# Banded attention: where the softmax's exponential, negation and sum are done, head by head on ScalarE

## What is computed

```python
idx = jnp.arange(T)[:, None] - deltas[None, :]
valid = idx >= 0
k_mod = k[:, :, idxc] * (1.0 + scale_embed)
scores = jnp.einsum('bhtd,bhtjd->bhtj', q, k_mod) * scale + pos_bias.T[None, :, None, :]
scores = jnp.where(valid[None, None], scores, jnp.finfo(scores.dtype).min)
attn = jax.nn.softmax(scores, axis=-1)          # over the 42 offsets, for each of 16 heads
out = jnp.einsum('bhtj,bhtjd->bhtd', attn, v_g) * if_gain[None, :, None, None]
return out.transpose(0, 2, 1, 3).reshape(B, T, C) @ w_out
```

## Time and profile before

| what | us |
|---|---|
| median of three runs | 3405.57 (3402.1 to 3410.08) |
| the profiled execution's own time | 3413.12 |
| its span | 3411.2 |
| steps of chunk 0 | 21.4 to 70.4 |
| steps of chunk 1, with the tail of chunk 0 | 70.4 to 142.9 |
| steps of chunk 2, with the tail of chunk 1 | 142.9 to 215.1 |
| steps of chunk 3, with the tail of chunk 2 | 215.1 to 284.3 |
| tail of chunk 3 alone | 284.3 to about 330 |

### The profile page before, as it was taken

How to read it: one execution, slowest core, us unless ns; L and a number is a source line. 1 busy time by engine, 2 the same in 40 slices (tenths; PEclk the granted TensorE clock), 3 DMA queues, 4 the chain that set the end, 5 groups by cost and what they waited for, 6 DMA issues and landing times. The chain is left out here.

```text
span 3411.2 us, 72275 instructions
## 1 busy us (share of the span) xinstructions
PE 3068.7 (90%) x29076; PEld 2124.1 (62%) x29076; DVE 1814.2 (53%) x4513; ACT 1181.2 (35%) x2319; POOL 995.6 (29%) x822
## 2 busy tenths in 40 slices
PE   8997999999988888889678999699997999889989
PEld 3434555555667865658345555489997886666656
DVE  7897544453334655433776666543333763455543
ACT  1223333332233431313326665222222652244433
POOL 1001443343102111426248878321111211104001
PEclk9998999999998999989889999799998999999989
DMA  4223000000222022527211110378886200121100
GB/s 156 65 75 100 10 9 18 9 9 0 54 58 26 7 52 74 150 79 255 70 33 31 32 31 19 110 292 329 328 328 230 77 2 13 37 73 51 49 14 19
DMA packets 174741, 287.70 MB, mean 84 GB/s; under 512 B 79393, under 2 KB 145025, under 8 KB 165102
## 3 DMA queue, kind: packets, MB, share of 16 engines
q1 hardware_dynamic: 166958, 263.07, 24.0%
q0 software_dynamic: 7488, 20.46, 1.8%
HBM read 245.07 MB, written 28.48 MB: 80 GB/s over the span
## 5 line engine op out<-in xcount | busy, mean ns | idle before, releaser
L2852 PE MATMUL ps<-L_ffn_xsT,arena 128*128 128x128 f32 x2584 | 304.0, 276 | 0.7 <-DVE L_ffn_xsT L2651 0.6
L2852 PEld LDWEIGHTS ps<-L_ffn_xsT,arena 128*128 128x128 f32 x2584 | 296.3, 193 | 3.6 <-DVE L_ffn_xsT L2651 3.5
L842 POOL TENSOR_TENSOR L_xattn_rn<-L_xattn_ss,mhalf 125x16 f32<-125x16 f32 (+1 forms) x64 | 185.8, 2903 | 257.3 <-DVE L_xattn_ss L905 257.3
L3534 POOL TENSOR_TENSOR L_xattn_pT<-L_xattn_pT,L_xattn_keep 125x678 int32<-125x678 int32 x128 | 190.4, 1509 | 62.6 <-ACT L_xattn_pT L3789 62.6
L162 POOL TENSOR_TENSOR rstd<-nsc,mhalf 112x4 f32<-112x4 f32 (+2 forms) x26 | 40.2, 1545 | 556.0 <-DVE nsc L155 555.0
L2750 ACT ACTIVATE L_ffn_silu<-ps,arena 128x128 f32<-128x128 f32 x280 | 102.9, 368 | 269.2 <-PE ps L2852 254.0
L2660 DVE SCALAR_TENSOR_TENSOR L_ffn_hT<-ps,arena,L_ffn_silu 128x128 f32<-128x128 f32 x280 | 98.0, 350 | 155.3 <-ACT L_ffn_silu L2750 155.1
L2529 POOL DMA_INDIRECT L_ffn_rows_out<-L_ffn_ys,L_ffn_dest x78 | 79.6, 1021 | 319.8 <-DVE L_ffn_ys L2669 304.1
L1019 PE MATMUL ps<-arena,L_xattn_cT 128*125 128x512 f32 x384 | 166.1, 592 | 0.0
L723 PE MATMUL ps<-L_attn_prod,arena 128*32 128x448 f32 (+28 forms) x672 | 153.5, 492 | 11.5 <-DVE L_attn_prod L523 10.9
L2865 PE MATMUL ps<-arena,L_ffn_hT 128*128 128x256 f32 x646 | 153.0, 381 | 5.5 <-ACT L_ffn_ys L2759 5.4
(11 more groups left out here) (616 smaller groups left out, 6753.2 us busy)
## 6 DMA issues: line engine op xcount, KB each, us to landing
arena<-in_L_ffn_up SPq DMA_DIRECT2D x35, 2056.0 KB, 8.1
arena<-in_L_ffn_down SPq DMA_DIRECT2D x35, 1152.0 KB, 8.6
L_xattn_ctxT<-in_ctxT SPq DMA_DIRECT2D x48, 375.0 KB, 3.7
arena<-in_L_ffn_up SPq DMA_DIRECT2D x43, 384.0 KB, 4.5
L_attn_a<-L_attn_skew SPq DMA_DIRECT2D x16, 784.0 KB, 5.2
L_xattn_ctx<-in_ctx SPq DMA_DIRECT2D x30, 375.0 KB
arena<-L_xattn_kp SPq DMA_DIRECT2D x64, 93.8 KB, 3.3
L_xattn_mask<-in_mask SPq DMA_DIRECT2D x32, 164.1 KB, 8.4
```

The costliest lines, as they stand in the source:

```text
L842: nc.gpsimd.tensor_tensor(rn[0:r, i], ss[0:r, i], core.mhalf[0:r, 0:H], ALU.pow).then_inc(po_r.step("root", i), 1)
L2852: ins = nc.tensor.matmul(ps[:, 2 + b % 4, half * TS:(half + 1) * TS], self.up(i % WU, k, half * HM + m), xsT[:, i % 2, k], start=(k == 0), ...
L3534: nc.gpsimd.tensor_tensor(p, p, keep[:, n % 2].unsqueeze(1).to_broadcast([SP_, 2, ST * TP]), ALU.mult).then_inc(po_e.step("kept", half), 1)
```

## The change

In the tails of chunks 0, 1 and 2 the subtraction over 672 elements is replaced by a negation of the 16 maxima. ACT takes the exponential as 16 instructions, one for each head, of 42 elements that lie 16 apart, with the negated maximum as bias and the sum accumulated into `den`. VectorE's sum is left out there. Before its first exponential of a chunk but the first, ACT waits for the reciprocal of the chunk before. `DIVIDE`, `TURN`, `ATTEND`, `SCALED`, `PROJECT` and `UPDATE` go four steps later, `MAX`, `SUB` and `EXP` stay. The last chunk's tail and its tables stay as they are.

```diff
-        ve_n = [Progress(core, f"vector_norm{u}", ("den", 1), ("rden", 1), ("wide", 1)) for u in range(U)]
+        ve_n = [Progress(core, f"vector_norm{u}", ("rden", 1), ("wide", 1)) for u in range(U)]
+        ve_f = [core.semaphore(f"vector_den{u}") for u in range(U)]
...
-            DIVIDE = {17 + 12 * u: u for u in range(U)}
-            TURN = {25 + 12 * (n // 4) + 2 * (n % 4): n for n in range(4 * U)}
-            ATTEND, SCALED, PROJECT = ({n + 12 * u: u for u in range(U)} for n in (33, 41, 42))
-            UPDATE = {min(50 + 12 * u, NI - 1): u for u in range(U)}
+            DIVIDE = {21 + 12 * u: u for u in range(U)}
+            TURN = {29 + 12 * (n // 4) + 2 * (n % 4): n for n in range(4 * U)}
+            ATTEND, SCALED, PROJECT = ({n + 12 * u: u for u in range(U)} for n in (37, 45, 46))
+            UPDATE = {min(54 + 12 * u, NI - 1): u for u in range(U)}
...
-                        dve.wait_ge(ve_n[u].sem, ve_n[u].at(c - 2, "den"))
+                        dve.wait_ge(ac_e.sem, ac_e.at(c - 2, "exp", u))
...
             def below(c, u):
                 dve.wait_ge(ve_m[u].sem, ve_m[u].at(c, "max"))
+                if c < NCH - 1:
+                    nc.vector.tensor_scalar(mx[:, u, :], mx[:, u, :], -1.0, None, ALU.mult).then_inc(ve_m[u].step("sub"), 1)
+                    return
...
                 dve.wait_ge(ac_e.sem, ac_e.at(c, "exp", u))
-                nc.vector.tensor_reduce(den[:, u, :], by_head(e[c % 2][:, u]), AX.X, ALU.add).then_inc(ve.step("den"), 1)
-                dve.wait_ge(ve.sem, ve.at(c, "den"))
+                if c < NCH - 1:
+                    core.stand(dve)
+                else:
+                    nc.vector.tensor_reduce(den[:, u, :], by_head(e[c % 2][:, u]), AX.X, ALU.add).then_inc(ve_f[u], 1)
+                    dve.wait_ge(ve_f[u], 1)
...
             def exponential(c, u):
                 act.wait_ge(ve_m[u].sem, ve_m[u].at(c, "sub"))
+                if c < NCH - 1:
+                    if c:
+                        act.wait_ge(ve_n[u].sem, ve_n[u].at(c - 1, "rden"))
+                    for h in range(H):
+                        row = by_head(e[c % 2][:, u])[:, h, :]
+                        ins = nc.scalar.activation(row, row, ACT.Exp, bias=mx[:, u, h:h + 1], accum_out=den[:, u, h:h + 1])
+                    ins.then_inc(ac_e.step("exp", u), 1)
+                    return
```

## The result

| | before | after |
|---|---|---|
| median of 5 runs, us | 3410.08 (3402.1 to 3415.9) | 3431.97 (3422.99 to 3437.66) |
| the profiled execution's own time, us | 3413.12 | 3422.99 |
| steps of chunk 1, us | 72.5 | 80.2 |
| steps of chunk 2, us | 72.2 | 81.2 |
| steps of chunk 3, us | 69.1 | 73.2 |

The ratio is 1.0061, with a 95% interval of 1.0045 to 1.0077: slower, by 21.9 us between the medians. The stage alone is 20.9 us longer (346.8 - 325.9). The two profiled executions differ by 9.9 us only, because stages that the change does not touch were some 11 us shorter in the profiled one of after; so from here on chunks and the end of the stage are compared, and ratios of medians where there are several runs.

The account below looks back on a forecast made before the run. PE and DVE were taken as nearly full, with faster DVE worth at most some 8.6 us each in chunks 1 and 2. Chunks sum 6.0 + 5.0 - 0.7 = 10.3 us more, 3416 forecast; range 3398 to 3429.

Parts of the forecast that it names:

- Price of a head: ACT, one activation of 42 spread elements plus accumulator read: 0.37 us (0.33 to 0.42); sixteen take 5.9 us.
- Step 1: Chunk 1: turned-input copies end at 88.6 behind the first exponential, so PE's q starts at 88.7 instead of 84.29.
- Step 2: Chunk 1: second exponential ends at 104.9, weight copies queue behind it, PE's third turn at 105.3 instead of 97.20.
- Step 3: Chunk 1, third turn to that of sequence 2: 22.1 us instead of 23.5; 1.4 of DVE's 5 us reach PE.
- Step 4: Chunk 1, sequence 2's third turn to next chunk's first product: 21.5 us instead of 22.2; chunk ends 6.0 later.
- Chunk 2: Same as chunk 1, but PE no longer lags into it, about 1 us back: 5.0 us later.
- Chunk 3: First exponential 10 us in, transfers 7.9, first turn some 24 in; 0.4 later on DVE, 1.1 less PE lag: -0.7.
- 1.1 less lag of PE: End of chunk 3: PE lags 1.1 us less, credited against 0.4 us later on DVE.
- Faster: DVE sets the pace: Exponentials hide and PE's waits on DVE in its own rows go: -10 us, 3395; chance 18%.
- Even: A head costs 0.33 us and the chain overstates adding waits: +2.6 or less, about 3408; chance 25%.
- Much slower: A head costs 0.42 us or more, accumulator reads not overlapping: +20, 3425, or beyond; chance 12%.
- signs: Activations about 0.28 us with reads between, q waiting on ACT, DVE waiting at `DIVIDE`, chunks 78, 77, about 70 us.

Follow-up runs that it names:

- version with right filling: Kernel after plus small constant products filling PE's stands: 16 before q, 8 before the third turn, in chunk 3 10 before the first turn; 1.0043, stage end 340.9.
- second profile of after: The kernel after run once more, unchanged, to see how far its stage repeats; ratio 1.0075, chunks of 80.3, 81.6 and 73.8, stage end 347.8.

## Why the prediction was wrong in size and right in direction

It said 10.3 us more, 3416; it came to 21.9 more, 3431.97, outside the range (3398 to 3429). Of the 16 us between these times 4.5 are before's own median, 3410.08 over five runs where the prediction had 3405.57 over three; with that median 21.9 more would have been 3427.5. The size is off all the same, 21.9 for 10.3. The stage gives 20.9.

What failed: the prediction let PE stand in front of q and of the turns and put the clock behind it at nothing, which was some 6 us; it took two credits, 1.0 for chunk 2 and 1.1 at the end, that did not come; and it had the first turn of chunk 3 too early. The cause of the slowdown, that ACT's exponentials stand in front of q and the weight copies, was right. By the steps of the text:

- **Price of a head**, 0.37 (0.33 to 0.42): 0.35, sixteen 5.6 where 5.9 stood. Right.
- **Step 1**, q at 88.7: 88.34, right in time. Missed: the clock. q took 3.19 us instead of 1.77, since PE had stood 3.95 us. The prediction wrote that PE stands and put no price on what follows.
- **Step 2**, third turn at 105.3: 106.08. In the version with right filling it came at 104.58, so the clock was 1.5 of it, and without the clock the step would have been 0.7 early (two exponentials at 5.6).
- **Step 3**, 22.1 us to the third turn of sequence 2: 22.3 (128.41). Of DVE's relief only a little reaches PE, as said. That the sum is so near is partly luck. From the end of the third exponential to the start of the fourth it took 6.8 us (115.17 to 122.00) where 5.9 stood, and the terms written there, 0.85, 0.58, 0.75, 1.04 and 1.8, make 5.0 only; shorter exponentials and a sooner last turn made up for it.
- **Step 4**, 21.5 us to the end, 2.5 of them waits of DVE: 22.2, with 0.78 + 0.62 + 1.94 = 3.3 of waits (22.8 in the version with right filling). Chunk 1 is 7.7 longer, not 6.0.
- **Chunk 2**, "PE no longer lags into it: about 1 us back": did not happen. The first exponential starts 11.0 us after the chunk's first product before and after, and the filled version's chunk 2 is 6.0 longer than before's, the sum without the credit. With the clock, lower for 6.8 + 3.4 us here, that makes 9.0 instead of 5.0.
- **Chunk 3**, +0.4 on DVE: +4.1. Wrong was the time of the first turn: "some 24 us in", measured 25.8. The first exponential starts 11.0 us in, before (226.03 - 215.06) and after, where the prediction read 10. And the transfers took longer: 9.2 us from the exponential's end to the first turn (257.62 - 248.39), where 7.9 stood. The score copy behind the first exponential, missed too, is not what held this turn: PE stood again, for the read back. ACT's timeline of the kernel before, the first exponential of chunk 3:

```profile
226.03 0.77 ACT L598 ACTIVATE arena<-arena 112x672 f32<-112x672 f32 x1
```

  SP's timeline of the kernel after and of before shows where the 1.3 went:

```profile
248.56 0.30 SPq L394 DMA_DIRECT2D L_attn_skew<-arena  x1
248.92 0.42 SPq L395 DMA_DIRECT2D L_attn_skew<-arena  x1
252.64 0.30 SPq L401 DMA_DIRECT2D L_attn_a<-L_attn_skew  x1
```

```profile
227.22 0.42 SPq L394 DMA_DIRECT2D L_attn_skew<-arena  x1
229.66 0.30 SPq L400 DMA_DIRECT2D L_attn_a<-L_attn_skew  x1
```

  The read back follows the second write to the skewed buffer after 3.7 us instead of 2.4 (3.3 in the version with right filling, 4.1 in the second profile of after). The packets of the trace show the core fetching instructions meanwhile: one such packet of 16 KB, from 250.47, took 1.08 us, and the write's last small packets came from 251.1 to 251.6. Late writes go with such fetches in all traces. The 16 traces of this text hold 192 of these writes in the steps of chunks 1 to 3; of 132 without a fetch in the first 2.3 us the read back followed after 2.4 to 2.5 us in all but one (2.7); of 60 with one, it took 2.6 to 4.1 in 39. So it is no price of the heads themselves: with the tables alone shifted it once took 3.8 too. That the fetch delays the write is not shown by an experiment.
- **"1.1 less lag of PE"** at the stage's end: the tail took 41.8 instead of 41.7. Did not happen.

The account of the missing 10.6 us (20.9 - 10.3), with the filled version as the stage without the lower clock: chunk 1 is 0.8 clock and 0.9 steps (without the lower clock steps 3 and 4 were 1.5 longer, the third turn 0.7 sooner); chunk 2 is 3.0 clock and 1.0 credit; chunk 3 is 1.9 clock and 1.8 the rest, nearly all of it the first turn (in the filled version 25.4 us in); the tail 1.2 credit. The clock is 5.7 of it, the credits 2.2, the rest 2.7. Two of these were knowable from the trace of before: it shows the lower clock from 288.7 us, in the last tail where PE waits, and the first exponential of chunk 3 at 226.03.

**The rivals.** *Faster: DVE sets the pace* had about the right price for relief (-10; measured -12.9 alone) and fell by its own condition: at 0.35 us a head the exponentials do not hide. *Even* needed 0.33 us a head. *Much slower*, +20 to 3425, met the size but not the cause: a head did not cost 0.42. That is luck. What was foreseen as signs came: reads between the activations, q on a wait for ACT, DVE's wait at `DIVIDE` four times in chunk 1; DVE's busy time fell by 27.8 us over the three windows (29 said). Foreseen wrongly were the chunks, 78, 77 and 70 against 80.2, 81.2 and 73.2, and the length of one activation, 0.28 against 0.36 (its row overlaps that of the read).

## What to carry to other kernels

Work moved to an engine that is idle in sum is not free when that engine serves others in order: price the length of the moved piece at each place where something queues behind it, not its share of the span. Ask next whether the piece can stay one instruction; here a common bias gave ACT the subtraction for 0.09 us a sequence, where the sixteen heads took 4.8 more than one exponential with the sums and 3.4 without. And where a step makes PE stand, look in the trace for what its clock did where it stood before, and put that into the sum.

## What was not expected of the hardware

- With PE standing 3.95 us the granted clock was 0.50 from 87.8 to 91.2 us, and the first q took 3.19 us instead of 1.77; with the stand filled by small products it took 1.77.
- The accumulator's read takes 0.19 us in the profile but adds 0.09 from start to start (0.35 with, 0.26 without).
- The maximum over 672 elements side by side to one value took 845 ns, over 16 groups of 42 spread elements 1286 ns. Which part is the spread and which the grouping was not tried.
- The small second write to the skewed buffer was followed by the read back after 2.4 to 2.5 us in 131 of the 132 cases without an instruction fetch beside it, and after up to 4.1 with one.
